# Cross attention with top-32 selection and a ternary feed forward: long rows for the context, rank-major candidates in shrinking searches, the last two tiles singly, all queues laid anew

## The reference, cut to what matters

```python
# x: 1x2048x256, ctx: 1x1601x256, fp32; biases are random, not zero
h = layernorm(x)
q, k, v = h @ Wq.T + bq, ctx @ Wk.T + bk, ctx @ Wv.T + bv
s = q @ k.T / 16                                  # 2048 x 1601
s = keep the 32 largest of each row, -inf elsewhere
x = x + softmax(s) @ v @ Wo.T + bo
h = layernorm(x)
h = bitlinear(h, w1, b1)     # rmsnorm, 8-bit rounding per row, ternary weights, 256 -> 1024
h = gelu(h)
x = x + bitlinear(h, w2, b2) # the same, 1024 -> 256
```

## Time and profile before

| | us |
|---|---|
| median of 3 runs | 314.02 (313.54 to 315.88) |
| profiled execution, its own time | 317.03 |
| its span, first to last instruction | 315.0 |
| PE busy | 283.6 (90%) |
| DVE busy | 246.0 (78%) |
| ACT busy | 208.0 (66%) |
| POOL busy | 130.2 (41%) |

### The profile page before, as it was taken

One profiled execution on the slowest core, in us unless ns is written; L12 is line 12 of the kernel. 1 busy time (PEld: TensorE's weight loads), 2 busy tenths in 40 slices (PEclk: granted clock), 3 DMA queues, 4 the chain that ended last, 5 costly groups with the idle time before them and its releaser, 6 DMA issues. The chain is left out here.

```text
span 315.0 us, 5565 instructions
## 1 busy us (share of the span) xinstructions
PE 283.6 (90%) x1640; PEld 246.8 (78%) x1640; DVE 246.0 (78%) x974; ACT 208.0 (66%) x317; POOL 130.2 (41%) x223
## 2 busy tenths in 40 slices
PE   8798997999999699999899989998999999798425
PEld 8697996899789598998698879887898888566114
DVE  2363498688999779989998999899989998963511
ACT  0554466545758874997399649855985796386452
POOL 4024601097863177127721863185316043305330
PEclk9889997999999999999999999999999999979957
DMA  7971001000100110002001100110001001000000
GB/s 182 315 280 33 3 2 32 0 16 7 50 2 17 37 50 0 3 17 86 1 1 41 61 2 17 50 37 0 19 19 33 3 17 33 20 0 1 33 0 33
DMA packets 14124, 12.23 MB, mean 39 GB/s; under 512 B 3853, under 2 KB 13646, under 8 KB 14094
## 3 DMA queue, kind: packets, MB, share of 16 engines
q1 hardware_dynamic: 13278, 11.09, 11.4%
q0 software_dynamic: 272, 0.79, 0.9%
q10 hardware_dynamic: 544, 0.00, 0.1%
HBM read 9.77 MB, written 2.10 MB: 38 GB/s over the span
## 5 line engine op out<-in xcount | busy, mean ns | idle before, releaser
L382 PE MATMUL bank<-vo,pT 128*128 128x257 f32 (+1 forms) x416 | 101.7, 386 | 2.2 <-ACT pT L857 1.9
L382 PEld LDWEIGHTS bank<-vo,pT 128*128 128x128 f32 (+1 forms) x416 | 75.9, 193 | 14.6 <-ACT pT L857 3.8
L1064 DVE MAX8 cand<-s_sb 128x8 f32<-128x50 f32 (+1 forms) x512 | 61.9, 196 | 8.1 <-ACT s_sb L807 5.2
L807 ACT ACTIVATE s_sb<-score 128x400 f32<-128x400 f32 x64 | 31.5, 507 | 36.1 <-PE score L235 36.0
L235 PE MATMUL score<-k_high,q_low 128*128 128x400 f32 (+1 forms) x128 | 51.1, 399 | 0.0
L235 PE MATMUL score<-k_low,q_high 128*128 128x400 f32 (+1 forms) x128 | 44.2, 345 | 0.0
L235 PE MATMUL score<-k_high,q_high 128*128 128x400 f32 (+1 forms) x128 | 44.1, 344 | 0.0
L857 ACT ACTIVATE pT<-bank 128x512 f32<-128x512 f32 x64 | 32.1, 515 | 16.0 <-PE bank L243 16.0
L243 PE MATMUL bank<-ident,e_all 128*128 128x128 f32 (+1 forms) x208 | 33.4, 283 | 1.3 <-ACT pT L857 0.7
L243 PE MATMUL bank<-ident,y 128*128 128x128 f32 x160 | 23.5, 289 | 11.3 <-ACT y L888 9.8
L1099 DVE SCALAR_TENSOR_TENSOR e_all<-s_sb,best,e_all 128x1601 f32<-128x1601 f32 x16 | 30.8, 1922 | 2.7 <-ACT e_all L849 2.7
(11 more groups left out here) (132 smaller groups left out, 514.0 us busy)
## 6 DMA issues: line engine op xcount, KB each, us to landing
x_in<-in_x SPq DMA_DIRECT2D x16, 128.0 KB, 2.3
w_sb<-in_L_ffn_w SPq DMA_DIRECT2D x2, 1024.0 KB, 11.9
x_res<-in_x SPq DMA_DIRECT2D x16, 128.0 KB, 2.1
out<-o_sb SPq DMA_DIRECT2D x16, 128.0 KB, 1.7
ctx_sb<-in_ctx SPq DMA_DIRECT2D x3, 512.0 KB, 10.1
b_bc<-in_L_ffn_b POOLq DMA_DIRECT2D x1, 512.0 KB, 8.2
w_q<-in_L_xattn_Wq SPq DMA_DIRECT2D x1, 256.0 KB, 3.3
w_k<-in_L_xattn_Wk SPq DMA_DIRECT2D x1, 256.0 KB, 4.7
```

The lines of the kernel that those rows point to most:

```text
L382: ins = pe.matmul(bank[:, 0:DV], pT[0:n, t % 2, b * P:(b + 1) * P], vo[0:n, b, :], start=(b == 0), stop=(b == SB - 1))
L807: act.activation(s_sb[:, t % 2, at:at + n], score[c][:, 0:n], ACT.Copy).then_inc(s_copied, 1)
L1064: ins = dve.max(cand[:, t % 2, 8 * k:8 * k + 8], s_sb[:, t % 2, k * PIECE:end])
```

## The change

- The first 1536 rows of the context are loaded so that each partition gets 12 consecutive rows (4 in each of 3 loads) instead of every 128th row. The order of the context rows, and so which scores share a piece of 50, is another; the attention is a sum over them and doesn't depend on it. Wq, Wk and their biases are loaded with two adjacent rows per partition, Wk and both biases from the ACT queue; x comes after the second context load. ACT does one tiny activation before its first wait.
- `cand` is rank-major (the 32 firsts, then the 32 seconds, and so on). The four searches look at the first 2, 4, 6 and 8 ranks alone (64, 128, 192, 256 elements), and values are struck out in place; `cand_left` is gone. The count that leads to the selection anew is now over 8 (only the last 8 of the 32 are left), the 8th of a piece still weighs 33.
- Tiles 14 and 15 go through the feed forward singly: their scales are made on DVE but for the root, which POOL takes; rounding of y1 on DVE; `turn_y1_tile` and `take_y1_tile` for half a bank.
- The bank that a PE job gets is that of its group which was taken longest ago, over all groups.
- Weight mean and ternary weights are made in the head instead of rounds 0 and 1.
- The orders of all five queues are laid anew. The core of the diff:

```diff
+DEPTH = (2, 4, 6, 8)
-            last[group] = (last[group] + 1) % len(group)
-            k = group[last[group]]
+            k = min(group, key=lambda b: latest[b])
+            latest[k] = len(place)
...
-            w_load("k", Wk, wk_in)
+            sp.dma_start(W_rows["q"][:, :, :], Wq.rearrange("(p c) d -> p c d", c=DC)).then_inc(wq_in, 16)
             for k in range((SB - 1) // CTX_PIECE):
                 lo, hi = k * CTX_PIECE, (k + 1) * CTX_PIECE
                 sp.dma_start(ctx_sb[:, lo:hi, :],
-                             ctx_rows[lo * P:hi * P, :].rearrange("(b p) d -> p b d", p=P)).then_inc(ctx_in[k], 16)
-                if k == 0:
+                             ctx_rows[0:(SB - 1) * P, :].rearrange("(p b) d -> p b d", b=SB - 1)[:, lo:hi, :]).then_inc(ctx_in[k], 16)
+                if k == 1:
                     load_x(0)
...
-                    ins = dve.max(cand[:, t % 2, 8 * k:8 * k + 8], s_sb[:, t % 2, k * PIECE:end])
+                    ins = dve.max(cand[:, t % 2, k:CAND:PIECES], s_sb[:, t % 2, k * PIECE:end])
-                dve.max(best[:, u, k, :], cand_left[:, u, :] if k else cand[:, u, :]).then_inc(topk_step[u], 1)
+                dve.max(best[:, u, k, :], cand[:, u, 0:DEPTH[k] * PIECES]).then_inc(topk_step[u], 1)
-                dve.match_replace(cand_left[:, u, :], best[:, u, k, :], cand_left[:, u, :] if k else cand[:, u, :],
-                                  LOWEST).then_inc(topk_step[u], 1)
+                found = cand[:, u, 0:DEPTH[k] * PIECES]
+                dve.match_replace(found, best[:, u, k, :], found, LOWEST).then_inc(topk_step[u], 1)
-                with dve.If(largest > TOPK):
+                with dve.If(largest > TOPK // ROUNDS):
...
+            # POOL, the rounds
+            for r in range(4):
+                row_scales_2(r + 1)
+                normalise(r + 4, 1)          # if live
+                row_scales_1(r + 2)
+                keep_residual(r + 2, 1)
+                quantise_1(r + 2, 0)
+                quantise_1(r + 2, 1)
+                split_queries(r + 4)         # if live
+                residual(2 * r + 6)
+                residual(2 * r + 7)
+                normalise_scale(r + 5)       # if live
+                normalise(r + 5, 0)          # if live
+                keep_residual(r + 3, 0)
+            row_scales_2(5)
+            keep_residual(6, 0)
...
+            # ACT, a round (the conditions left out)
+            take_y2(2 * r - 4, 1)
+            take_y2(2 * r - 3, 0)
+            copy_scores(2 * r + 1, 1)
+            take_y2(2 * r - 3, 1)
+            copy_scores(2 * r + 1, 2)
+            take_weights(2 * r, 0)
+            copy_scores(2 * r + 1, 3)
+            take_weights(2 * r, 1)
+            take_queries(r + 1)
+            exp_all(2 * r + 1)
+            take_weights(2 * r, 2)
+            take_weights(2 * r, 3)
+            take_y1(r - 1)
+            copy_scores(2 * r + 2, 0)
+            gelu(2 * r - 2)
+            copy_scores(2 * r + 2, 1)
+            take_weights(2 * r + 1, 0)
+            squares(2 * r - 2)
+            copy_scores(2 * r + 2, 2)
+            copy_scores(2 * r + 2, 3)
+            take_weights(2 * r + 1, 1)
+            gelu(2 * r - 1)
+            take_weights(2 * r + 1, 2)
+            take_weights(2 * r + 1, 3)
+            squares(2 * r - 1)
+            exp_all(2 * r + 2)
+            copy_scores(2 * r + 3, 0)
+            quantise_2(2 * r - 2)
+            quantise_2(2 * r - 1)
+            take_y2(2 * r - 2, 0)
...
+            # DVE, a round (the conditions left out)
+            largest_count(2 * r)
+            attended(2 * r - 1)
+            release(2 * r)
+            centre(2 * r - 2)
+            moments(2 * r - 1)
+            output(2 * r - 4)
+            candidates(2 * r + 1, 1)
+            centre(2 * r - 1)
+            candidates(2 * r + 1, 2)
+            candidates(2 * r + 1, 3)
+            best_8(2 * r + 1, 0)
+            next_8(2 * r + 1, 1)
+            next_8(2 * r + 1, 2)
+            next_8(2 * r + 1, 3)
+            output(2 * r - 3)
+            count(2 * r + 1)
+            weigh(2 * r + 1)
+            ln1_stats(r + 2)
+            largest_count(2 * r + 1)
+            attended(2 * r)
+            release(2 * r + 1)
+            hidden(2 * r - 2, 0)
+            hidden(2 * r - 2, 1)
+            candidates(2 * r + 2, 0)
+            hidden(2 * r - 1, 0)
+            hidden(2 * r - 1, 1)
+            candidates(2 * r + 2, 1)
+            gelu_max(2 * r - 2)
+            candidates(2 * r + 2, 2)
+            candidates(2 * r + 2, 3)
+            gelu_max(2 * r - 1)
+            best_8(2 * r + 2, 0)
+            next_8(2 * r + 2, 1)
+            next_8(2 * r + 2, 2)
+            next_8(2 * r + 2, 3)
+            moments(2 * r)
+            count(2 * r + 2)
+            weigh(2 * r + 2)
+            candidates(2 * r + 3, 0)
```

871 lines of the change are left out of this document (577 added, 294 removed).

## The result

The kernel after takes 371.2 us (median of 4 runs, 370.18 to 372.33) against 313.8 for the kernel before (4 runs, 313.54 to 315.88): a ratio of 1.181, 95% interval 1.175 to 1.188. Slower, as forecast, but by 57 us and not by 10, and far outside the range of 303 to 330. The profiled execution has a span of 368.4 us.

A forecast was written before the change was run, and what follows sets the result against it. Rounds bound by DVE, busy 28.7 of 30.5 us. Span 315.0 -5.9 (head) -2.0 (rounds 1, 2) +6.3 (rounds 3 to 6) +2.6 (last pair) +8.9 (tail) = 324.9, taken over to 323.9 us; range 303 to 330.

The forecast's parts named there:

- The rounds: Rounds 3 to 6: 28.7 us of DVE work plus waits of 0.7, 0.3 and 2.4, 32.1 each, +6.3 in all.
- The mechanism (2): On POOL keep_residual(r, 0), ahead of row_scales_2(r-1), waits for bn_stats; output stalls DVE 2.4 us (N: tile 2r+2's neg_max).
- up to 2 us a round: PE idles from about N+1.7 to N+7.4; a fallen clock could add this much, left to the range.
- Nobody catches up, since DVE is the bound: At output in each round: DVE stalls 2.4 us with all of its list queued behind, and the delay stays.
- Head: Up to tile 2's first maximum: fold some 1.7 us sooner, first candidates at 32.8, maximum at 62.3 instead of 68.2, -5.9 us.
- Rounds 1 and 2: The first two rounds, 63.0 us before, would take 28.9+32.1 = 61.0, -2.0 us.
- Shorter searches: DVE's searches in each tile: 0.86 us a tile less, 1.7 a round, net 1.4 after about 0.1 at three steps.
- Last pair: Up to the end of tile 15's weigh: a 4.6 us wait at output(10), 23.5 us instead of 20.9, +2.6.
- Tail: From T0, the end of tile 15's weigh: 33.4 us, but 49.7 with 17.4 of selection anew, against 40.8, +8.9.
- The POOL wait is hidden: Rival, chance 0.28: in the rounds the place of keep_residual costs nothing, rounds 29.7, 307.1 us.
- The selection anew doesn't run: Rival, chance 0.10: no selection anew in tile 15, but the POOL wait stays; tail 33.4, 307.6 us.
- The rule on the table load: Before each round's exponential: the skill's drain of about 1.38 us, some 8 us in all, left out; load costs 1.28.

The follow-up runs named there:

- a1: The kernel after with POOL's keep_residual(r, 0) put back behind row_scales_2(r-1): 331.5 us.
- a4: The kernel after with 40 transposes that nobody reads put on PE in each round, where it is idle: 358.1 us.
- d3: c1 with ln1_stats ahead of odd tiles' weigh on DVE, and on POOL the even residual ahead of row_scales_1, the odd one behind normalise: 301.56 us.
- d2: The kernel after with DVE's first output of a round moved behind the odd tile's searches: 385.3 us.
- b2: The kernel before with POOL's keep_residual(r, 0) put ahead of row_scales_2(r-1), as in the kernel after: 319.8 us.
- a6: a1 with the key bias issued ahead of Wk on ACT's queue: 326.6 us.
- b3: The kernel before with the context loaded in the new order of rows (long rows) alone: 334.1 us.
- a2: The kernel after with the context loaded in the old order of rows: 350.6 us.
- c1: a3 with the key bias ahead of Wk and spread_value_bias ahead of normalise_scale(0): 304.65 us.
- b1: The kernel before with the shorter searches alone, all orders as before: 311.6 us.
- a3: The kernel after with both the edits of a1 and a2, POOL order undone and old context rows: 311.0 us.

## Why the prediction was wrong

Its span was 324.9 us, the measured one 368.4: 43.5 too little. By its own steps:

**The rounds: the step that failed.** Predicted 32.1 us each, measured 37.1 (rounds 2 to 6 together 185.7 against 160.5): 25.2 of the 43.5 us. The mechanism (2) is right, place and releaser too: with the one order undone (a1) the rounds are 30.4. The term that was mis-sized is its stall, put at 2.4 us: the order costs 6.7, of which 6.2 are the wait at `output` and 0.5 the held `count`. `down` ends at N+15.5, not N+11.1. 1.5 of these 4.4 us are in the six steps of the scales: the sum took 2.65 us from the earlier trace rows, where no `weigh` lay beside them, and the new order puts the root into `weigh` (2.24 instead of 0.71). 2.6 are the clock (a4); 0.3 are not placed. DVE comes to `output` at N+9.5, not N+8.7, 0.5 of it by `count`, which the sum had at 0.41. The text had both the idle stretch and the half clock, but bounded them by "up to 2 us a round" and left them out of the sum, although the tail in the earlier trace rows showed the lower clock behind such waits. They weren't a bound but the likely case. The other 0.7 of a round is the round without the wait, 30.4 against 29.7: the sum had `weigh` at 1.80 us, and in odd tiles POOL's `split_queries` holds it to 2.88. Where that is mended (d3), the rounds are 29.9 in the mean.

**"Nobody catches up, since DVE is the bound"** stood for the wrong reason. The delay is carried by every in-order queue (d2), not by DVE. And "DVE at N+8.7" against "`down` at N+11.1" was the right comparison: b2 shows that where DVE comes at N+12.6 the same late scales cost no wait there.

**Head.** 62.3 predicted for the first maximum of tile 2, 71.09 measured: 8.8 us. The prediction let the fold end 1.7 us sooner and moved Wk to another queue at no cost. It missed what stands behind Wk there: the key bias, the operand that the fold waits for. Between after and a6 the first candidates differ by 4.1 us. The longer rows were to help too and did not (b3; after against a2). By the prediction's own sign, a head that gains less than 3 us, it was wrong here: the head lost 3.0. It also wrote that PE's stall on `spread_value_bias` goes; it stays, at 3.03 us, since POOL has it behind `normalise_scale`, which waits for DVE until 26.47, and two `normalise`. With both mended, and in the old row order, c1 has its first candidates at 31.9 and the first maximum of tile 2 at 63.0 us: the head that was forecast, but not of this kernel. Between first candidates and that maximum lie 31.1 us in every version made from after, and 31.0 in the kernel before, where the forecast had 29.5.

**Rounds 1 and 2.** Round 1, without `output`, 28.9 against 30.4: 1.5 us, the same base that came out too low.

**Shorter searches.** 1.4 us a round net, by b1 1.0. The searches themselves are as forecast, 0.80 us a tile against 0.86, and MATCH_REPLACE8 does scale as MAX8 (409 to 209 ns from 256 to 64 elements). That the net is close is partly luck: the 0.3 taken off were for missing fillers, and what is missing is 0.5 of a held `count`.

**Last pair.** 23.5 against 25.5; without the wait 18.7, in a1 18.5. The wait was 4.6 (18.7 and 4.6 make 23.3; the text wrote 23.5) and is 7.4. Here it is the clock alone. The scales are ready at N+9.9, as forecast, with the root at 0.75 us, but PE has stood idle for 6.4 us:

```profile
294.40 0.75 POOL L827 TENSOR_TENSOR row<-row,minus_half 128x2 f32<-128x2 f32 x1
```

```profile
298.42 1.97 PE L248 MATMUL bank<-ident,y 128*128 128x128 f32 x8 [6.40 <-ACT y L1058]
```

a4 has no transposes in this gap, and its last pair is as long, 25.6.

**Tail.** 49.7 against 55.7. The selection anew is 17.0 us of DVE, forecast 17.4, at T0+4.6 instead of T0+3.1; it adds 17.2 (55.7 against 38.5 in a2). The rest was to be 33.4 and is 38.2 in a3: all that is new in the tail, the single tiles among it, brings 2.3 to 2.6 us against the tails of b1 and before and not 7. `weighted(15)` ends 14.8 us behind T0 there, against 12.1 before: ACT, in order, takes tile 15's weights behind the gelus of pair 6. This part of the tail was not tried by itself.

**The rivals.** "The POOL wait is hidden" is refuted in this kernel and true in the orders of before (b2). "The selection anew doesn't run" is refuted by the trace. **The rule on the table load**: each of the 14 table loads in the trace of after is 1.28 us long and is followed within 0.02 us by its exponential or gelu, without a drain; by the rows it was right to leave it out.

## What to carry to other kernels

Price a wait together with what it sets off: TensorE stood idle for 4.3 us in each round, the first work behind it ran at half clock, and here that was over a third of the loss of a round. Ask of an order not only what waits but what covers it, since the same line cost 0.4 us in one order and 6.7 in another. When steps of two engines are laid side by side, list DVE's two-input operations (`weigh`, `count`) against POOL's work, and when a load changes its queue, look at the small operand behind it.
